# The causal mask as constant rows of the query and key stacks of an attention and expert block

## The reference

```python
Q = _apply_rope(proj(Wq, bq), cos, sin)      # 16 heads of 8, after a modulated layer norm
K = _apply_rope(proj(Wk, bk), cos, sin)
scores = jnp.einsum('bhqd,bhkd->bhqk', Q, K) * (1.0 / jnp.sqrt(jnp.asarray(hs, x.dtype)))
causal = jnp.tril(jnp.ones((T, T), dtype=bool))
scores = jnp.where(causal, scores, jnp.asarray(-10000000000.0, x.dtype))
att = jax.nn.softmax(scores, axis=-1)
y = jnp.einsum('bhqk,bhkd->bhqd', att, V)
```

## Time and profile before

| | us |
|---|---|
| median of 3 runs | 484.22 |
| lowest and highest | 483.38, 491.34 |
| profiled execution, its own time | 483.1 |
| its span | 481.3 |
| TensorE busy, 2844 matmuls | 385.9 |
| VectorE busy | 288.7 |
| ScalarE busy | 248.4 |
| GpSimd busy | 115.1 |

### The profile page before, as it was taken

One profiled execution on the slowest core, in us unless ns is written; L12 is line 12 of the kernel. 1 busy time (PEld: TensorE's weight loads), 2 busy tenths in 40 slices (PEclk: granted clock), 3 DMA queues, 4 the chain that ended last, 5 costly groups with the idle time before them and its releaser, 6 DMA issues.

```text
span 481.3 us, 7596 instructions
## 1 busy us (share of the span) xinstructions
PE 385.9 (80%) x2844; PEld 172.7 (36%) x2844; DVE 288.7 (60%) x587; ACT 248.4 (52%) x301; POOL 115.1 (24%) x157
## 2 busy tenths in 40 slices
PE   0543989978889978999899799989989995338994
PEld 0510334543344444434454344345542123112122
DVE  7473885729866696787586777774691212592211
ACT  1020005670024686875449768654587981038981
POOL 7018000034014020533242024332201323101322
PEclk9875557998557999999999899999998999559999
DMA  8014000114000172553005445500042530043540
GB/s 288 0 35 97 1 2 3 34 42 60 1 5 3 33 97 81 136 149 58 25 2 77 55 122 146 145 8 26 12 55 82 149 122 22 1 67 83 142 125 22
DMA packets 26848, 31.44 MB, mean 65 GB/s; under 512 B 6454, under 2 KB 17718, under 8 KB 26678
## 3 DMA queue, kind: packets, MB, share of 16 engines
q1 hardware_dynamic: 23740, 28.84, 24.9%
q0 software_dynamic: 3072, 2.13, 2.6%
HBM read 3.47 MB, written 1.05 MB: 9 GB/s over the span
## 4 chain that ended last, share of the span: by engine, by line
PE 52%; DVE 16%; ACT 10%; issue 9%; DMA 7%; SPq 3%; POOL 1%; POOLq 0%; ACTq 0%; DVEq 0%
PE misc L995 21%; PE big L995 16%; PE acc L995 12%; ACT ring L579 8%; DVE mx L796 6%; DMA tstack<-tp 4%; PE misc L1014 2%; SPq L389 2%; DMA gm<-wT 2%; DVE xn L742 1%; ACT qk_turned L587 1%; DMA q_block<-qk_turned 1%; SPq L313 1%; POOL gm L523 1%; ACT yT L619 1%
## 5 line engine op out<-in xcount | busy, mean ns | idle before, releaser
L579 ACT ACTIVATE ring<-big 128x1024 f32<-128x1024 f32 (+1 forms) x224 | 197.7, 935 | 160.7 <-PE big L995 159.7
L796 DVE TENSOR_REDUCE mx<-misc 128x1 f32<-128x512 f32 (+7 forms) x176 | 100.6, 591 | 34.0 <-PE misc L995 30.0
L995 PE MATMUL misc<-k_dense,q_block 128*128 128x512 bf16 (+7 forms) x256 | 82.5, 373 | 23.7 <-DMA q_block<-qk_turned 14.6
L995 PE MATMUL big<-tstack,w1s 128*128 128x512 bf16 x256 | 77.0, 395 | 20.0 <-DMA tstack<-tp 12.3
L995 PE MATMUL acc<-ring,cb 128*32 128x512 f32 x512 | 67.8, 604 | 2.6 <-DVE gm L911 2.1
L995 PEld LDWEIGHTS misc<-k_dense,q_block 128*128 128x128 bf16 x256 | 36.1, 147 | 85.7 <-DVE mx L796 61.2
L995 PE MATMUL big<-q_dense,k_block 128*128 128x512 bf16 (+7 forms) x256 | 60.9, 335 | 4.1 <-ACT ring L579 3.7
L911 DVE SCALAR_TENSOR_TENSOR gm<-acc,cb,gm 128x512 f32<-128x512 f32 x32 | 23.9, 747 | 52.6 <-DMA gm<-wT 27.2
L995 PE MATMUL misc<-later_key,identb 128*128 128x64 bf16 x256 | 50.5, 222 | 0.0
L523 POOL TENSOR_TENSOR gm<-osb,gm 128x512 f32<-128x512 f32 x16 | 20.4, 1276 | 125.7 <-DMA gm<-wT 63.7
L995 PEld LDWEIGHTS big<-q_dense,k_block 128*128 128x128 bf16 x256 | 35.4, 145 | 40.7 <-ACT ring L579 19.0
(11 more groups left out here) (137 smaller groups left out, 394.8 us busy)
## 6 DMA issues: line engine op xcount, KB each, us to landing
gm<-wT SPq DMA_DIRECT2D x64, 256.0 KB
tstack<-tp SPq DMA_DIRECT2D x24, 128.0 KB, 4.8
k_dense<-qk SPq DMA_DIRECT2D x24, 64.0 KB
k_block<-qk_turned POOLq DMA_DIRECT2D x48, 32.0 KB, 3.5
q_dense<-qk SPq DMA_DIRECT2D x24, 64.0 KB
ca<-in_pack_a SPq DMA_DIRECT2D x1, 1155.0 KB, 5.3
xs<-in_x SPq DMA_DIRECT2D x4, 256.0 KB, 7.9
q_block<-qk_turned SPq DMA_DIRECT2D x32, 32.0 KB
```

The source lines that it names most:

```text
L579: act.activation(dst, src, func, scale=scale).then_inc(s["ring_read"], 1)
L796: dve.tensor_reduce(mx[:, g, k:k + n, blk], src, AX.X, ALU.max).then_inc(s["misc_read"], 1)
L995: return pe.matmul(dst, lhsT, rhs, start=start, stop=stop)
```

## The change

Partitions 64 to 127 of all four stacks, zero before, get constants once, in the setup. In `k_dense` and `q_dense` they are the mask of a block, repeated for all blocks and head pairs; in `q_block` and `k_block` they are the identity of 64, for both heads and all blocks. The matmul of a diagonal block (64 columns) then contracts over all 128 partitions and its sum includes the mask. The rest of the row of blocks (w - 64 columns) is a matmul of its own over partitions 0 to 63 alone, so that no mask is added there. Where w is 64 there is only the diagonal one. The constants are copied by ScalarE (four copies, `lay_masks`), two before `turn(0)` and two behind it. The memsets of the stacks shrink to partitions 0 to 63, and the constants are built for partitions 64 to 127 only.

```diff
-            for t in (ident, identb):
-                pool.affine_select(out=t[:, :], in_=t[:, :], compare_op=ALU.not_equal, fill=1.0, base=0,
-                                   pattern=[[-1, P]], channel_multiplier=1).then_inc(s["shapes_ready"], 1)
...
-            pool.wait_ge(s["shapes_ready"], 7)
-            pool.memset(k_block[:].rearrange("r p a t -> r (p a t)").bitcast(F32), 0.0).then_inc(s["zeroed"], 1)
-            pool.memset(q_block[:].rearrange("r p a t -> r (p a t)").bitcast(F32), 0.0).then_inc(s["zeroed"], 1)
+            pool.affine_select(out=ident[:, :], in_=ident[:, :], compare_op=ALU.not_equal, fill=1.0, base=0,
+                               pattern=[[-1, P]], channel_multiplier=1).then_inc(s["shapes_ready"], 1)
+            pool.wait_ge(s["shapes_ready"], 2)
+            rows = slice(BLK, P)
...
+            pool.wait_ge(s["shapes_ready"], 5)
+            pool.memset(k_block[0:BLK].rearrange("r p a t -> r (p a t)").bitcast(F32), 0.0).then_inc(s["zeroed"], 1)
+            pool.memset(q_block[0:BLK].rearrange("r p a t -> r (p a t)").bitcast(F32), 0.0).then_inc(s["zeroed"], 1)
...
+            def lay_masks(dense, later, block):
+
+                act.copy(dense[BLK:P].rearrange("r p (s t) -> r (p s) t", t=BLK),
+                         later[BLK:P].unsqueeze(1).to_broadcast([BLK, NP * NS, BLK])).then_inc(s["masks_laid"], 1)
+                act.copy(block[BLK:P].rearrange("r p a (q s) -> r (p a) q s", s=NS),
+                         identb[BLK:P].unsqueeze(1).unsqueeze(3).to_broadcast([BLK, 2 * NP, BLK, NS]))\
+                   .then_inc(s["masks_laid"], 1)
+
...
-            act.wait_ge(s["shapes_ready"], 1)
+            act.wait_ge(s["shapes_ready"], 5)
             load_table(ACT.Exp)
+            lay_masks(k_dense, later_key, q_block)
             turn(0)
+            lay_masks(q_dense, earlier_query, k_block)
...
-                dve.memset(t[:].rearrange("r p t -> r (p t)").bitcast(F32), 0.0).then_inc(s["cleared"], 1)
+                dve.memset(t[0:BLK].rearrange("r p t -> r (p t)").bitcast(F32), 0.0).then_inc(s["cleared"], 1)
...
+            def scored(dst, block, dense, free, diagonal):
+
+                if free is not None:
+                    at, w = free
+                    matmul(dst[:, at:at + w], block[0:BLK], dense[0:BLK, at:at + w])
+                return matmul(dst[:, diagonal:diagonal + BLK], block, dense[:, diagonal:diagonal + BLK])
...
-                        matmul(dst[:, w * j:w * j + w], blocks(q_block, p, blk), k_dense[:, p, 0:w], stop=False)
-                        ins = matmul(dst[:, w * j + at:w * j + w], identb[:, :], later_key[:, :], start=False)
+                        ins = scored(dst[:, w * j:w * j + w], blocks(q_block, p, blk), k_dense[:, p, 0:w],
+                                     (0, at) if blk else None, at)
...
-                    matmul(big[:, bk, col:col + w], blocks(k_block, p, blk), q_dense[:, p, at:T], stop=False)
-                    ins = matmul(big[:, bk, col:col + BLK], identb[:, :], earlier_query[:, :], start=False)
+                    ins = scored(big[:, bk, col:col + w], blocks(k_block, p, blk), q_dense[:, p, at:T],
+                                 (BLK, w - BLK) if w > BLK else None, 0)
...
+            pe.wait_ge(s["masks_laid"], 2)
             maxima(here, MAXIMA)
             pe.wait_ge(s["ones_loaded"], 16)
+            pe.wait_ge(s["masks_laid"], 4)
```

More of the change, by code:

```diff
@@ L182, in build @@
         minus_half = sb("minus_half", [P, TT])
-        identb = sb("identb", [P, P], BF16)
+        identb = sb("identb", [P, BLK], BF16)
         later_key = sb("later_key", [P, BLK], BF16)
@@ L253, in build @@
             "a_loaded", "b_loaded", "x0_loaded", "x_loaded", "w1_loaded", "ones_loaded",
-            "zeroed", "cleared", "marks", "tabled", "shapes_ready", "exp_ready", "abs_ready", "sil_ready", "mod_ready",
+            "zeroed", "cleared", "marks", "tabled", "shapes_ready", "masks_laid", "exp_ready", "abs_ready", "sil_ready", "mod_ready",
             "gates_filled", "setup_link", "modb_ready", "w1_ready",
@@ L432, in _ @@
         def _(pool):
-            for t in (later_key, earlier_query, ident, identb):
+            for t in (later_key, earlier_query, identb, ident):
                 pool.memset(t[:, :], 0.0)
@@ new lines, in _ @@
+            rows = slice(BLK, P)
+            pool.affine_select(out=later_key[rows], in_=later_key[rows], compare_op=ALU.is_ge, fill=MASKED,
+                               base=0, pattern=[[-1, BLK]], channel_multiplier=1).then_inc(s["shapes_ready"], 1)
+            pool.affine_select(out=identb[rows], in_=identb[rows], compare_op=ALU.not_equal, fill=1.0, base=0,
+                               pattern=[[-1, BLK]], channel_multiplier=1).then_inc(s["shapes_ready"], 1)
+            pool.affine_select(out=earlier_query[rows], in_=earlier_query[rows], compare_op=ALU.is_ge,
+                               fill=MASKED, base=0, pattern=[[1, BLK]],
+                               channel_multiplier=-1).then_inc(s["shapes_ready"], 1)
@@ L1005, in _ @@
             ins.then_inc(s["gates_filled"], 1)
-            pe.wait_ge(s["shapes_ready"], 7)
+            pe.wait_ge(s["shapes_ready"], 5)
             def filled(ins):
```

## The result

The changed kernel takes 608.96 us (median of 4 runs, 605.57 to 609.9) against 484.14: 1.256 times, 95% interval 1.250 to 1.262. It is slower by 125 us; the forecast was 564. The profiled execution has a span of 606.9 us.

The account below looks back on a forecast made before the run. TensorE's instruction stream was taken to bound the softmaxes and the expert stages with maxima. 64 us there and 16 in the maxima of batches 0 and 1 made +80: 483.1 + 80 = 563, median 564 us, range 474 to 590.

Parts of the forecast that it names:

- What bounds the kernel: TensorE's stream of instructions sets the pace of the four softmaxes and of the two expert stages that carry maxima.
- the 85% I took: Part of TensorE's added time in warm softmax and expert stretches put on the path: 64 of 75 us.
- The weights' shape: Score and maxima matmuls: each switch between 64 and 128 rows costs 0.16 us, making the sum +1.74 us a warm set.
- Fewer columns: Score and maxima matmuls: the masks' 64 columns go away, -0.16 us a set of the eight widths.
- that case, a rival: TensorE's score and maxima matmuls: rows switch freely, so the kernel gets faster, 477 us (474 to 480); chance 0.30.
- Maxima of batches 0 and 1: These maxima run alone at half clock, with 0.20 us a shape change: +8 us each, +16.
- Experts with maxima: Two stretches between softmaxes, holding experts and the maxima of batches 2 and 3: 24 us more.
- The constants: Setup: ScalarE's copies take 10.3 us, within 12.77 us of idle time ahead of `turn(0)`, so they add nothing.
- That GpSimd free earlier changes nothing: Setup: three selects fewer free GpSimd 0.7 us early, in a stretch where nothing waits for it.
- The four softmaxes: The score passes of the four batches, taken at full clock: 40 us more.
- the clock rival: Warm softmax and expert stretches: gaps drop half of 150 us to 1.2 GHz, 30 us more, 595 us; chance 0.07.

## Why the prediction was right or wrong

*What bounds the kernel*: right. TensorE's instruction stream sets the softmaxes and the expert stretches with maxima. In the latter 24.4 us came through of the 27.8 worked out (16 x 1.74), 88%, near the 85% I took; in the softmaxes the share on the path can't be told from the clock's.

*The weights' shape*: right, and the deciding step. No row of before had a matmul over 64 rows; the price was taken from the change of columns, 0.16 us, and the changed kernel's rows show 0.09 and 0.06. The Trainium skill, page "TensorEngine Tiling (Array Packing)", section Key Properties, has the rule that a change of tiling mode drains the engine. The trace agrees in that the next load waits for the end of the stream and 0.09 us more; it starts 0.08 us ahead of the modelled end of the matmul (311.35 against 311.43), so that the array is empty by then isn't shown.

*Fewer columns*: right in size where it can be seen alone, and lucky in the sum. With the changes of shape away the kernel gains 8 us (476.27), where the forecast for that case, a rival, was 477. The third and fourth softmaxes, at full clock in both kernels, are 1.1 us shorter each (34.6 for 35.7, 31.0 for 32.1), and 8 x 0.16 x 85% is 1.1. But 3.0 us come ahead of the first exponential and 1.3 in the maxima of batch 1, for which the forecast had 0.5, and 2.7 in the second softmax, where the clock is 0.97 instead of 0.88; the expert stretches give 0.5 together instead of 2.2.

*Maxima of batches 0 and 1*: mis-sized, 12.5 for 16 us. At half clock a change costs 0.14 + 0.02, not 0.14 + 0.06: the matmul waits only 0.02 us for its weights there.

*Experts with maxima*: right, 24.4 for 24. At clock 0.95, against 1.00 and 0.97 before, most of it is the price.

*The constants*: right for the copies. The profile of the changed kernel has the copies at 3.60 and 7.01 us, 10.6 for the 10.3 forecast, inside the idle time:

```profile
18.12 3.60 ACT L570 COPY k_dense<-later_key 64x4096 bf16<-64x4096 bf16 x1
21.63 7.01 ACT L572 COPY q_block<-identb 64x8192 bf16<-64x8192 bf16 x1
30.64 3.01 ACT L594 COPY qk_turned<-qk 128x512 bf16<-128x512 bf16 x3 [2.00 <-DVE qk L767]
```

That GpSimd free earlier changes nothing was wrong, by 0.7 us. It makes two selects fewer, not three, and its second big memset ends at 9.52 us instead of 10.23. VectorE has an operation on 128x4 elements beside it that lasts until just then (before first, then changed):

```profile
6.72 3.51 POOL L454 MEMSET q_block<- 128x4096 f32 x1
7.60 2.66 DVE L675 TENSOR_SCALAR sil<-sil 128x4 f32<-128x4 f32 x1
...
6.02 3.50 POOL L452 MEMSET q_block<- 64x4096 f32 x1
7.58 1.98 DVE L684 TENSOR_SCALAR sil<-sil 128x4 f32<-128x4 f32 x1
```

All behind it, `turn(0)` too (30.64 for 31.34), comes 0.7 us earlier. The first maxima start 1.4 us earlier (42.50 for 43.92); where the other 0.7 comes from isn't shown. These 1.4 us are the larger part of the -2.1 in the table.

*The four softmaxes*: this is the step that failed. I summed them at full clock (40 us, measured 90.8) and made the clock's fall a rival of 0.07, priced at 30 us. It is what happened: at full clock a batch would lose 8 x 1.74 - 14 x 0.16 = 11.7 us, 47 in all with everything on the path; the measured 90.8 leave 44 us for the clock, an estimate that rests on the sum of 11.7. Two things were misjudged. The profile of before held the warning that the clock is not a given: batches 0 and 1 enter their softmax from half clock, and it has to come back within it. In the changed kernel it doesn't, for 94% of both. And I looked for the cause only in the gaps. That weights of 64 rows hold the clock down too had no row in the trace of before. With the first matmuls over 64 rows the half-clock time in the softmaxes is 156 us, with changes by columns alone 62. Why the two together do more than their sum isn't shown. Neither is what in short rows or in gaps the clock answers to.

The range ended at 590, below the 595 of the clock rival itself. The 590 doesn't follow from its terms either: 75 us with all on the path and 20 at half clock give 484 + 95 = 579. The price and the falling clock come from the same instructions; taken as one case, all on the path and with the rival's 30 us, they give 609, which is what was measured, though with 44 us of clock and less from the rest.

## What to carry to other kernels

Price a matmul by the shape its neighbours have: each switch between weight shapes (rows or columns) cost 0.13 to 0.16 us here, and two of them were to save the 0.027 us of 64 columns. If a contraction needs fewer rows than its neighbours, leave the rest zero and contract over all 128, as the kernel before does. Putting matmuls of one shape together got back 87 of the 125 us, not all. When a change thins out TensorE's work, forecast the stretches again at half clock, above all those that begin there, and take both effects as one case.

## What the runs showed of the hardware

- A change from 128*128 to 64*128 weights and back costs about as much as one from 128*128 to 128*64 or 128*32: about 0.09 us from the end of the stream to the next weight load, and at full clock 0.06 us until the matmul where the next weights are strided, 0.01 to 0.03 where they are not (0.14 and 0.02 at half clock).
- Matmuls over 64 rows, with no change of shape among them, kept the granted clock at 0.68 and 0.65 in softmaxes where matmuls over 128 rows with zeros in the rest had 0.97 and 0.88, and made the kernel 23 us slower (508.71 against 485.67). A contraction over all 128 rows, 74 of them zero, did not do that. The pace at either clock is the same over 64 rows as over 128 (a pitch of 0.28 and 0.48 us at w = 512).
- With the matmuls of both passes over 64 rows the run time scatters by 2.5% (4 runs from 509.48 to 522.15), and the mean granted clock with it (0.845 to 0.816). With those of the scores alone it doesn't (507.41 to 510.14).
- A VectorE operation on 128x4 elements, next to a GpSimd memset of 3.5 us, ended only with it: it lasted 2.66 us in the kernel before and 1.98 in the changed one, where the memset ended 0.7 us earlier.
